# Six runs of four scatters, each begun at a step of the dense part, in place of three runs of eight

## The chip, the cores and the metric

The kernel runs on one core of a Trainium2 chip. The metric is the device time in microseconds of one execution; the time of the kernel before is the median of three.

## The reference

The input x is 8 batches of 256 rows, 128 wide. Three sub-layers follow, each on a layer norm of x without weights, each added back:

```python
x = x + 0.5 * ffn(layernorm(x))
x = x + attention(layernorm(x))
x = x + 0.5 * ffn(layernorm(x))
```

The FFN is a mixture of 8 experts with 2 chosen for each row: `gelu(x @ w1[e]) * (x @ v1[e])`, 352 wide, then `@ w2[e]`, weighted by the two largest of the softmax of `x @ router_w`, plus a bias. The attention has 16 heads of width 8, rotary positions and a linear distance term; it bears on the change only by what it waits for.

## The kernel before, in words

The rows are 16 tiles of 128 (`NT`). In the first FFN the first four tiles (`DT`) take the dense way: all eight experts are computed for them and weighted by the gate, 0 for an expert that was not chosen. The other twelve are routed: their normalised rows are scattered to a table in HBM (`xs0`), sorted by expert, each row twice (k is 0 or 1), and computed afterwards in blocks of 128 rows of one expert.

The engines run programs of their own, written out by hand, and meet by semaphores. Each engine executes in program order, so a wait holds everything behind it on that engine.

**The dense part** is a loop of 24 steps (i, three for each expert). In a step PE computes da and dv (`dense_up`, lines 1434 to 1436, two times three matmuls of 512 columns), ACT takes the gelu of da (`dense_gelu`, L842, waits for `da_full` and `dhid_done`), DVE multiplies it by dv (`dense_hid`, L1107, increments `dhid_done`; every fourth result goes to `vaug`, the others to `scr`; the third step of each expert is 96 rows high), and two steps later PE multiplies by w2 (`dense_down`, L1444). Between the steps stand LN, transposes, the routing of chunks c = 1 to 3 of four tiles (the last operation of each is `pos_done`, L1015), the block table of the first FFN on DVE (its last operation, `tab_e`, L1050), and ACT's near_high. After step 23 PE first does `xbT(0)` (L1462, transposes of the first three blocks), for which it waits until three block loads have landed, and only then the last two `dense_down`.

**GpSimd** in that time, in program order: LN's small operations, the first `add_ffn_bias` (half of the FFN's bias added to four tiles of xres, L593), then for c = 1 to 3 the eight scatters of a chunk (L531, two for each tile, each an indirect DMA of 128 rows), then `zero_scatter(0)` (L573 and L576, rows of zeros behind each expert's last row), then the other three bias adds. After that it waits for `scat1`, `zero_landed`, `spare_landed` and `tab`, clears the buffers of the attention with six memsets (L649, `zero_done`), sets `vaug` to 1 (L651, after `down_done` 24), and does `rstd_of(1, 0)` and `rstd_of(1, 1)` (L516 to L521), the attention's LN of the first tiles, which waits for DVE's statistics; then one scatter of results for each block (L538).

**SP** waits at `rows_there(0)` for the table, the scatters (`scat1`) and the zero rows (`zero_landed`) and then loads blocks (L418), six ahead. After the load for block 7 it waits for `zero_done`. **ACT** uses the result of `rstd_of(1, 0)` (`nmr_done`) in `ln_at(0)` (L736) after block 2. The bias adds are needed by `combine`, in the attention part.

Of the kernel before, what the change touches and what calls it, by code (L numbers as in the profile page):

```python
# [28 lines left out]
DT = 4  # L29
# [48 lines left out]
CHUNKS = [(4, 4), (2, 8)]  # L78


ROUTED = [CHUNKS[0][1], SPLIT, CHUNKS[1][1]]


# [38 lines left out]
def macaron(nc, x, small_w, w1, v1, w2, ffn_bias, proj_b, slopes, ident, dist, dist_t, rope, expert_ids,  # L122
            far, ones_rows, out):
    ctx = ExitStack()
    with ctx:
# [5 lines left out]
        def sem(name):  # L131
            return ctx.enter_context(nc.semaphore(name))

        def sems(name, n):
            return [ctx.enter_context(nc.semaphore(f"{name}{i}")) for i in range(n)]
# [21 lines left out]
        xn1 = qk_f[:, 6096:6096 + (NT - DT) * 2 * XW].rearrange("p (t k w) -> p t k w", t=NT - DT, k=2)  # L157
# [115 lines left out]
        def routing_bank(c):  # L273
# [32 lines left out]
        scat1, scat2 = sem("scat1"), sems("scat2", 2)  # L306
# [3 lines left out]
        da_full, dv_full, dgelu_done, dhid_done, down_done, dacc, xd_step, gd_step = (sem(n) for n in (  # L310
            "da_full", "dv_full", "dgelu_done", "dhid_done", "down_done", "dacc", "xd_step", "gd_step"))
# [20 lines left out]
        def rt_at(r, c, step):  # L332


            per = 2 * CHUNKS[r][0] + 6
            return c * per - (3 if r == 0 and c else 0) + (per if step is None else step)
# [13 lines left out]
        def loaded(engine, table, g, most):  # L350
            _, vals = nc.values_load_multi_w_load_instructions(
                table[0:1, g, :], engines=[engine], min_val=0, max_val=most,
                skip_runtime_bounds_check_because="the table's values are held in range by how it is made")
            return vals[0:GS]
# [156 lines left out]
        def _(pool):  # L511
# [11 lines left out]
            def scatter(r, c, src, landed, tiles=None):  # L523

                T = CHUNKS[r][0]
                p = 2 if r and c >= SPLIT else r
                pool.wait_ge(pos_done[r], c + r)
                pool.wait_ge(again_done[r], c + r)
                for t in tiles or range(c * T, (c + 1) * T):
                    for k in range(2):  # L530
                        nc.gpsimd.indirect_dma_start(  # L531
                            out=xs[p][:, :], out_offset=bass.IndirectOffsetOnAxis(ap=pos[:, k, t:t + 1], axis=0),
                            in_=src(t, k), in_offset=None).then_inc(landed, 16)
# [35 lines left out]
            def zero_scatter(p):  # L569
                r, zeros = min(p, 1), zero_rows2 if p else zero_rows1  # L570
                pool.wait_ge(zstep[r], 18 if p == 2 else 9)
                pool.wait_ge(numbered, 4 if p else 3)
                nc.gpsimd.indirect_dma_start(  # L573
                    out=xs[p][:, :], out_offset=bass.IndirectOffsetOnAxis(ap=zpos[:, 0, :], axis=0),
                    in_=zeros[:, ZG, :], in_offset=None).then_inc(zero_landed[r], 16)
                nc.gpsimd.indirect_dma_start(  # L576
                    out=xs[p].rearrange("(g z) d -> g (z d)", z=ZG),
                    out_offset=bass.IndirectOffsetOnAxis(ap=zpos[:, 1, :], axis=0),
                    in_=zeros[:, 0:ZG, :].rearrange("p z w -> p (z w)"), in_offset=None).then_inc(zero_landed[r], 16)
# [7 lines left out]
            def add_ffn_bias(r, q):  # L587
                if q == 0:
                    if r == 0:
                        nc.gpsimd.tensor_scalar(hbias[:, :], hbias[:, :], 0.5, None, ALU.mult).then_inc(half_done, 1)  # L590
                        pool.wait_ge(half_done, 1)
                pool.wait_ge(xn_done[2 * r], 4 * q + 4)
                nc.gpsimd.tensor_tensor(xres[:, 4 * q:4 * q + 4, :], xres[:, 4 * q:4 * q + 4, :],  # L593
                                        hbias[:, None, :].broadcast_to([P, 4, D]), ALU.add).then_inc(bias_added, 1)
# [41 lines left out]
            nc.gpsimd.tensor_scalar(slope8[:, :], slope8[:, :], 8.0, None, ALU.mult).then_inc(slope_done, 1)  # L636
            pool.wait_ge(numbered, 3)
            for c in range(1, 4):
                scatter(0, c, lambda t, k: xn1[:, t - DT, k, :], scat1)
            zero_scatter(0)  # L640
            for q in range(1, 4):
                add_ffn_bias(0, q)

            pool.wait_ge(scat1, 16 * 2 * (NT - DT))
            pool.wait_ge(zero_landed[0], 32)
# [323 lines left out]
        def _(dve):  # L969
# [51 lines left out]
            def block_table(p, step):  # L1021
# [3 lines left out]
                if step == 0:  # L1025
                    dve.wait_ge(rt[r], rt_at(r, ROUTED[p], 0))
                    nc.vector.tensor_tensor(T.tgt, end[:, :, None].broadcast_to([P, E, 16]), thr[:, :, :], ALU.is_gt
# [25 lines left out]
            def zero_rows(p):  # L1053


                r, at = min(p, 1), 9 if p == 2 else 0
                dve.wait_ge(rt[r], rt_at(r, ROUTED[p], 0))
                if p:
# [706 lines left out]
```

## Time and profile before

| | us |
|---|---|
| median of 3 runs | 485.16 |
| lowest and highest | 484.56, 487.63 |
| profiled execution, span from first to last instruction | 502.7 |
| PE busy, in the profiled execution | 441.0 |
| DVE, ACT, POOL busy | 311.2, 248.2, 237.4 |

The profiled execution is a single one, recorded by the hardware profiler. Its own time beyond the span isn't given; the span alone is 17.5 us more than the median. Rows give times in us from the span's start. "idle before" is what an engine waited before an instruction, with what ended the wait; "remote" and "issue" stand where the profile knows no instruction of this core that did.

### The profile page before, as it was taken

The page shows a single profiled execution, that of the slowest core. Times are in us where ns is not written, and L with a number is a line of the kernel's source. Part 1 is how long each engine was busy: PE and PEld are TensorE (multiplying, and loading weights), DVE is VectorE, ACT ScalarE, POOL GpSimd, SP SyncE. Part 2 cuts the span into 40 slices and gives each one's busy share as a digit, 9 for nine tenths or more (in the row PEclk, how much of TensorE's full clock was granted, in tenths as well). Part 3 has the DMA queues.
Part 4 walks back from the last instruction along what each step waited for, and adds up shares of the span by engine and source line. Part 5 has one row for each costly group of instructions (what it writes and reads, how often), then busy time and mean ns, then how long its engine had stood idle before and what let it go on. Part 6 is the DMA issues. An engine that isn't in the chain of part 4 may idle for free.

```text
span 502.7 us, 10906 instructions
## 1 busy us (share of the span) xinstructions
PE 441.0 (88%) x3447; PEld 369.0 (73%) x3447; DVE 311.2 (62%) x935; ACT 248.2 (49%) x585; POOL 237.4 (47%) x321
## 2 busy tenths in 40 slices
PE   1998859899999898699999999999779969999990
PEld 1877648788899775577777777777459958888880
DVE  3765645976867485295959586756526744544672
ACT  4744434436444456255556565555465524554541
POOL 7365658556453413044454545432525467534441
PEclk9999959999999999899999999999999989999997
DMA  8971111122331010230212120200112223122522
GB/s 236 290 116 38 48 58 33 50 75 75 91 85 54 30 48 15 71 85 17 60 50 61 47 63 30 64 24 3 70 37 61 64 60 96 53 65 72 171 80 78
DMA packets 50633, 35.51 MB, mean 71 GB/s; under 512 B 5754, under 2 KB 47706, under 8 KB 50538
## 3 DMA queue, kind: packets, MB, share of 16 engines
q1 hardware_dynamic: 45140, 23.90, 18.9%
q0 software_dynamic: 4784, 10.54, 6.3%
q8 instruction: 30, 0.49, 0.4%
q10 hardware_dynamic: 656, 0.40, 0.3%
q14 instruction: 23, 0.19, 0.1%
HBM read 15.37 MB, written 13.01 MB: 56 GB/s over the span
## 4 chain that ended last, share of the span: by engine, by line
PE 65%; DVE 9%; issue 8%; ACT 5%; POOL 4%; DMA 3%; another core or an unknown queue 2%; ACTq 1%; SPq 1%; POOLq 0%; DVEq 0%
PE bank L1490 9%; PE bank L1483 6%; PE bank L1587 5%; PE bank L1472 5%; PE bank L1473 4%; PE bank L1474 4%; PE bank L1626 4%; PE bank L1611 4%; PE bank L1444 3%; PE bank L1590 2%; PE bank L1591 2%; PE bank L1462 2%; PE bank L1614 2%; PE bank L1434 2%
## 5 line engine op out<-in xcount | busy, mean ns | idle before, releaser
L538 POOL DMA_INDIRECT yp<-scr,dest x77 | 76.5, 994 | 90.8 <-ACT scr L770 71.1
L877 ACT ACTIVATE stage<-bank 128x512 f32<-128x512 f32 x128 | 74.6, 597 | 72.6 <-PE bank L1615 63.7
L1263 DVE TENSOR_REDUCE nm<-bank 128x2 f32<-128x512 f32 x128 | 84.0, 685 | 38.4 <-PE bank L1591 35.8
L1490 PE MATMUL bank<-wd,scr 128*128 (+1 forms) x462 | 64.9, 277 | 1.3 <-ACT scr L763 1.3
L1472 PE MATMUL bank<-wu,xbT 128*128 x154 | 63.1, 410 | 2.1 <-DVE xbT L1129 1.8
L1137 DVE COPY scr<-bank 128x256 f32<-128x256 f32 x77 | 32.5, 422 | 51.5 <-PE bank L1483 22.8
L1490 PEld LDWEIGHTS bank<-wd,scr 128*128 128x128 f32 (+1 forms) x462 | 60.7, 193 | 1.8 <-issue 1.7
L1587 PE MATMUL bank<-qk_rows 126*128 126x256 bf16 x256 | 50.8, 280 | 4.9 <-DMA qk_rows<-lev 4.2
L1611 PE MATMUL bank<-qk_rows 128*128 128x256 bf16 x256 | 50.3, 279 | 3.7 <-DMA qk_rows<-wd 3.0
L1473 PE MATMUL bank<-wu,xbT 128*128 x154 | 50.8, 330 | 0.0
L1474 PE MATMUL bank<-wu,xbT 128*128 x154 | 50.8, 330 | 0.0
L783 ACT ACTIVATE scr<-bank 128x352 f32<-128x352 f32 x77 | 35.7, 463 | 29.1 <-PE bank L1474 21.7
L1483 PE MATMUL bank<-idn,scr 128*128 128x128 f32 (+1 forms) x231 | 40.1, 283 | 10.0 <-ACT scr L770 8.7
L1614 PE MATMUL bank<-near_hi,idn_r 128*128 128x256 f32 x128 | 47.3, 369 | 0.0
L1590 PE MATMUL bank<-near_hi,idn_r 128*128 128x256 f32 x128 | 47.0, 367 | 0.0
L1156 DVE TENSOR_TENSOR scr<-bank,scr 128x352 f32<-128x352 f32 x77 | 40.1, 521 | 9.4 <-ACT scr L783 2.1
L763 ACT ACTIVATE scr<-bank 96x128 f32<-96x128 f32 x77 | 21.0, 273 | 47.9 <-DVE scr L1137 33.9
L1483 PEld LDWEIGHTS bank<-idn,scr 128*128 128x128 f32 (+1 forms) x231 | 25.1, 138 | 23.0 <-issue 14.7
L1615 PE MATMUL bank<-near_lo,idn_r 128*128 128x256 f32 x128 | 36.0, 281 | 0.0
L1591 PE MATMUL bank<-near_lo,idn_r 128*128 128x256 f32 x128 | 35.8, 280 | 0.0
L531 POOL DMA_INDIRECT xs<-qk_rows,pos x28 | 27.4, 980 | 15.9 <-issue 9.9
L1626 PE MATMUL bank<-stage,vaug 128*9 128x256 f32 x512 | 34.2, 385 | 0.4 <-ACT stage L877 0.4
(218 smaller groups left out, 949.3 us busy)
## 6 DMA issues: line engine op xcount, KB each, us to landing
qk_rows<-lev SPq DMA_DIRECT2D x96, 64.0 KB
scr<-xs SPq DMA_DIRECT2D x77, 64.5 KB
stage<-yp SPq DMA_DIRECT2D x8, 256.0 KB, 3.2
scr<-yp SPq DMA_DIRECT2D x6, 256.0 KB, 3.1
stage<-in_w SPq DMA_DIRECT2D x8, 176.0 KB, 3.4
stage<-in_v SPq DMA_DIRECT2D x8, 176.0 KB, 4.3
xs<-qk_rows SPq DMA_DIRECT2D x3, 451.5 KB
yp<-scr,dest POOLq DMA_INDIRECT x77
```

The source lines that it names most:

```text
L538: nc.gpsimd.indirect_dma_start(out=yp[PHASE[n]][:, :], out_offset=bass.IndirectOffsetOnAxis(ap=dest[:, n:n + 1], axis=0), in_=ysb[:, n % Y ...
L877: nc.scalar.activation(probs[:, g % RING, kt, 2 * (hp % 2):2 * (hp % 2) + 2, :], psS2[(b * 16 + j) % 3][:, :].rearrange("p (h n) -> p h n" ...
L1263: nc.vector.tensor_reduce(nm[:, qt, 2 * hp:2 * hp + 2], psS1[i % 2][:, :].rearrange("p (h n) -> p h n", h=2), AX.X, ALU.max, negate=True). ...
L1472: nc.tensor.matmul(dst, hi, moving(n, a), start=True, stop=False)
L1473: nc.tensor.matmul(dst, lo, moving(n, a), start=False, stop=False)
L1474: nc.tensor.matmul(dst, hi, moving(n, a + 2 * F), start=False, stop=True).then_inc(done, 1)
L1483: i = nc.tensor.transpose(ph[n % len(ph)][0:w, k * P:(k + 1) * P], hid[:, n % 2, f:f + w], idn[:, :])
L1490: i = nc.tensor.matmul(ph[n % len(ph)][:, 3 * P:4 * P], hTs[0:w, n % 2, k * P:(k + 1) * P], wd[0:w, bass.ds(experts[n], 1), k, :].rearrang ...
L1587: nc.tensor.matmul(o[:, j * N:(j + 1) * N], qs[b % RING][0:S1_ROWS, h, qt * P:(qt + 1) * P], ks[b % RING][0:S1_ROWS, h, :], start=(j == 0) ...
L1590: nc.tensor.matmul(o, idn_r[:, :], near_hi[0][:, 2 * hp:2 * hp + 2, :], start=False, stop=False)
L1611: nc.tensor.matmul(o[:, a * N:(a + 1) * N], ks[b % RING][0:S2_ROWS, h, kt * P:(kt + 1) * P], qs[b % RING][0:S2_ROWS, h, :], start=(a == 0) ...
L1614: nc.tensor.matmul(o, idn_r[:, :], near_hi[1][:, 2 * hp:2 * hp + 2, :], start=False, stop=False)
```

## The change

The eight scatters of a chunk are split into two runs of four (two tiles each). Six runs, called turns 0 to 5 here, result. Each but the first waits until `dhid_done` has reached 5 + 3 x turn, that is 8, 11, 14, 17 and 20: dense steps 7, 10, 13, 16 and 19 are then done on DVE. After the first run of each chunk stands the chunk's bias add, so the three bias adds no longer follow the zero scatter. The zero scatter follows the sixth run directly.

```diff
+RUN_AT, RUN_STEPS = 5, 3
...
             for c in range(1, 4):
-                scatter(0, c, lambda t, k: xn1[:, t - DT, k, :], scat1)
+                for half in range(2):
+                    turn = 2 * (c - 1) + half
+                    if turn:
+                        pool.wait_ge(dhid_done, RUN_AT + RUN_STEPS * turn)
+                    scatter(0, c, lambda t, k: xn1[:, t - DT, k, :], scat1, range(4 * c + 2 * half, 4 * c + 2 * half + 2))
+                    if half == 0:
+                        add_ffn_bias(0, c)
             zero_scatter(0)
-            for q in range(1, 4):
-                add_ffn_bias(0, q)
```

Before, GpSimd from the first scatter of the routed tiles to the first memset (xs0 is the sorted table in HBM, pos and zpos the positions that rows go to):

```order
L531 DMA xs0<-qk_rows,pos 19712x129 [waits again_done0,pos_done0,numbered]
L531 DMA xs0<-qk_rows,pos 19712x129 x7
L531 DMA xs0<-qk_rows,pos 19712x129 [waits again_done0,pos_done0]
L531 DMA xs0<-qk_rows,pos 19712x129 x7
L531 DMA xs0<-qk_rows,pos 19712x129 [waits again_done0,pos_done0]
L531 DMA xs0<-qk_rows,pos 19712x129 x7
L573 DMA xs0<-qk_rows,zpos 19712x129 [waits numbered,zstep0]
L576 DMA xs0<-qk_rows,zpos 2464x1032
L593 TENSOR_TENSOR xres<-xres,hbias 128x512 [waits xn_done_f1] x3
L649 MEMSET qk_rows 128x2048 [waits spare_landed,tab0,zero_landed0,scat1]
```

After, the same engine from the rest of the third run (turn 2) to the same memset:

```order
L532 DMA xs0<-qk_rows,pos 19712x129 x3
L594 TENSOR_TENSOR xres<-xres,hbias 128x512 [waits xn_done_f1]
L532 DMA xs0<-qk_rows,pos 19712x129 [waits again_done0,pos_done0,dhid_done]
L532 DMA xs0<-qk_rows,pos 19712x129 x3
L532 DMA xs0<-qk_rows,pos 19712x129 [waits again_done0,pos_done0,dhid_done]
L532 DMA xs0<-qk_rows,pos 19712x129 x3
L594 TENSOR_TENSOR xres<-xres,hbias 128x512 [waits xn_done_f1]
L532 DMA xs0<-qk_rows,pos 19712x129 [waits again_done0,pos_done0,dhid_done]
L532 DMA xs0<-qk_rows,pos 19712x129 x3
L574 DMA xs0<-qk_rows,zpos 19712x129 [waits numbered,zstep0]
L577 DMA xs0<-qk_rows,zpos 2464x1032
L654 MEMSET qk_rows 128x2048 [waits spare_landed,tab0,zero_landed0,scat1]
```

Each run of four has its own wait for `dhid_done` now, a bias add stands behind the first run of each chunk, and nothing is left between the zero scatter and the memset. The other engines' programs are unchanged.

## Rows read from the trace of the kernel before

**Rows 1.** Page: the span, and the granted clock of PE in 40 slices

```profile
span 502.7 us, 10906 instructions
...
PEclk9999959999999999899999999999999989999997
```

**Rows 2.** Waits, 13 to 93 us: who for whom, us in total, times, longest

```profile
ACT scr L842 <- remote: 14.6, 3, 7.0
...
PE bank L1434 <- issue: 6.6, 2, 4.9
...
PE bank L1434 <- ACT scr L842: 1.2, 1, 1.2
```

**Rows 3.** Timeline of GpSimd (start, us, engine, line, operation, tiles, count, idle before)

```profile
24.36 1.64 POOL L593 TENSOR_TENSOR xres<-xres,hbias 128x512 f32<-128x512 f32 x1
...
42.38 0.95 POOL L531 DMA_INDIRECT xs<-qk_rows,pos  x1 [3.63 <-DVE pos L1015]
...
54.87 0.96 POOL L531 DMA_INDIRECT xs<-qk_rows,pos  x1 [2.33 <-DVE pos L1015]
...
66.23 0.95 POOL L576 DMA_INDIRECT xs<-qk_rows,zpos  x1 [0.31 <-issue]
67.20 3.73 POOL L593 TENSOR_TENSOR xres<-xres,hbias 128x512 f32<-128x512 f32 x3
77.50 10.55 POOL L649 MEMSET qk_rows<- 128x2048 f32 x6 [6.57 <-DVE tab_e L1050]
90.24 0.82 POOL L651 MEMSET vaug<- 128x864 f32 x1 [2.18 <-PE bank L1444]
92.88 0.28 POOL L516 TENSOR_SCALAR rstd<-mv 128x2 f32<-128x2 f32 x1 [1.82 <-DVE mv L976]
...
94.64 0.24 POOL L516 TENSOR_SCALAR rstd<-mv 128x2 f32<-128x2 f32 x1
```

**Rows 4.** Timeline of ACT: the gelu of step 16, and ln_at(0)

```profile
66.99 0.60 ACT L842 ACTIVATE scr<-bank 128x512 f32<-128x512 f32 x1 [6.98 <-remote]
...
96.68 0.87 ACT L736 ACTIVATE stage<-xres,nmr,rstd 128x128 f32<-128x128 f32 x2
```

**Rows 5.** Timeline of PE: end of da(16), the resumption, xbT(0), the other long idle

```profile
60.73 0.39 PE L1436 MATMUL bank<-xbT,wu 128*128 128x512 f32 x1
...
67.64 0.74 PE L1434 MATMUL bank<-xbT,wu 128*96 128x512 f32 x1 [4.95 <-issue]
...
87.90 0.49 PE L1462 MATMUL bank<-idn,scr 128*128 128x128 f32 x3
...
411.23 0.87 PE L1483 MATMUL bank<-idn,scr 128*128 128x128 f32 x3 [4.39 <-ACT scr L770]
```

**Rows 6.** By stretch: busy PE, PEld, DVE, ACT, POOL; PEclk, DMA share, GB/s

```profile
62.00:68.00 6.00, 1.05 (x8) 0.86 (x7) 0.00 (x0) 1.01 (x3) 4.76 (x6) 0.77 0.18 63
68.00:76.00 8.00, 7.31 (x24) 5.43 (x24) 5.29 (x11) 3.20 (x8) 2.94 (x3) 0.53 0.13 52
```

**Rows 7.** Timeline of DVE: a cast, the table's last operation, dense_hid(19)

```profile
24.78 1.26 DVE L993 CAST ixf<-ix 128x8 f32<-128x8 uint32 x1
...
76.98 0.38 DVE L1050 TENSOR_REDUCE tab_e<-qk_rows 1x33 int32<-1x231 f32 x1
78.10 0.69 DVE L1107 TENSOR_TENSOR vaug<-bank,scr 128x512 f32<-128x512 f32 x1 [0.74 <-ACT scr L842]
```

**Rows 8.** Bytes moved, 40 slices each: of 67 to 77 us, then of 78 to 83

```profile
GB/s 0 0 17 429 396 429 429 380 33 0 0 0 0 0 0 0 0 0 0 0 0 0 0 0 0 0 0 0 0 0 0 0 0 0 0 0 0 0 0 0
...
GB/s 0 0 0 0 0 0 0 0 37 186 186 108 17 87 157 136 79 112 128 227 112 17 0 12 144 219 103 156 70 140 161 116 62 165 161 103 37 0 8 8
```

**Rows 9.** Timeline of SP: the first block loads

```profile
78.08 12.12 SPq L418 DMA_DIRECT2D scr<-xs  x7
```

**Rows 10.** Busy time by stretch: about 411 us, and the first expert blocks

```profile
410.00:418.00 8.00, 6.78 (x33) 6.64 (x33) 2.97 (x9) 2.54 (x8) 3.83 (x4) 0.57 0.34 116
88.00:100.00 12.00, 10.78 (x79) 9.66 (x77) 11.05 (x38) 5.06 (x15) 6.87 (x12) 1.00 0.20 52
```

## The prediction

> **What bounds the kernel now.** I read the page first: span 502.7 us, PE busy 88% of it [rows 1]. So PE's idle stretches and its slow-clock stretches are the only places where much can be won. The waits of the dense part (13 to 93 us) come next: ACT's gelu waits 14.6 us in three stretches for something that the profile can't name, the longest 7.0, and PE loses 6.6 us in two stretches and 1.2 in one behind it [rows 2]. GpSimd's timeline shows what goes on meanwhile: three unbroken series of indirect DMAs, eight scatters each, the second from 42.38 and the third from 54.87 us, the last with the two zero scatters right behind it [rows 3]. From 54.87 to 66.23 there are nine steps, so one scatter costs 11.36 / 9 = 1.262 us of GpSimd.
>
> The worst stall in detail: PE ends the last of da(16) about 61 us (its L1436 at 60.73), the gelu that needs it starts at 66.99, and PE, which needs that gelu, resumes at 67.64 after 4.95 us [rows 4, 5]. No semaphore of the kernel explains the 6 us: the gelu waits for da_full and dhid_done, both in. It happens only inside long series of scatters. Then the clock: PEclk 0.77 in 62 to 68 us and 0.53 in 68 to 76, that is mostly the 1.2 GHz level after 4.95 us without a matmul [rows 6]; 7.31 us of PE work there at 0.53 cost 7.31 x 0.47 = 3.4 us. After the two shorter idles of PE the clock stays full (nines in the page's PEclk row up to the slice of 62.8 to 75.4 us, a 5) [rows 1].
>
> **What the change does to the stalls.** Sum of what stands in the trace: 6.6 + 1.2 us of PE idle + 3.4 us of clock = 11.2 us. The new runs are four scatters, 4 x 1.262 = 5.0 us, with a bias add or a wait between. The stalls of before set in some 5 to 7 us into a series, so the trace of after should have none, or little, in the first five runs. Price if the stalls are real: -11.2 us.
>
> **What it adds.** The last run now waits for dhid_done 20, the end of dense_hid(19). That is the DVE row at 78.10 that writes vaug; it ends at 78.79 [rows 7]. From there, in the frame of before, where steps 19 to 23 run without a stall:
> - wake-up 0.2 us (estimate), four scatters and two zero scatters without a pause: 5 x 1.262 + 0.95 = 7.3. Together 7.5.
> - the zero scatter's data: its instruction at 66.23 ends at 67.18, its last bytes move at about 69.2 (ninth bin of 0.25 us after 67) [rows 3, 8]: 2.0.
> - SP stands at rows_there for zero_landed and then loads. Before, the table was the last to come: tab_e ends at 77.36, SP's first issue is at 78.08 [rows 7, 9]: 0.7.
> - three loads of 64.5 KB: the zero among the bytes at about 80.7 us ends the first three of six [rows 8, 9]: 80.75 - 78.08 = 2.7.
> Sum 12.9 us after dhid(19). PE wants these three tiles for xbT(0) at 87.90 [rows 5], 87.90 - 78.79 = 9.1 after it. Before, the loads lay there at about 81, 7 us early. Now PE stands for 12.9 - 9.1 = **3.8 us**, with the last two dense_down, dense_add and everything after them queued behind. All the slack of the rows' path is used, and 3.8 more.
>
> The second follower is GpSimd itself: six memsets of qk_f wait for zero_landed as well (10.55 us from 77.50), then vaug (0.82), then rstd_of(1, 0), which at 92.88 waited for DVE's statistics [rows 3]. From dhid(19): 9.5 (zero landed) + 10.6 + 0.9 + 1.7 for its four operations (the next group starts at 94.64) = 22.7, so nmr is there at 101.5; ACT used it at 96.68 [rows 4]. That is 4.8 us late, 1.0 beyond the 3.8 of PE; if PE's slow clock costs that 1.0 anyway it is hidden. Slack before: 92.88 against 91.06, 1.8 us. zero_done for SP's ones_rows has the same 10.6 us before it, but its readers come later still, behind the 3.8; I charge nothing.
>
> Clock after the new idle: nothing in the trace shows this place idle. Bounds: 0 (the idles of 1.6 and 1.2 us left the clock full) and 3.4 (the 4.95 us idle). The nearest row is the 4.39 us idle of PE before 411.23: the window from 410 to 418 us has 0.57 with PE busy 6.78 us [rows 5, 10], so 6.78 x 0.43 = 2.9 us. In the expert blocks PE is busy about nine tenths (10.78 of 12 us, rows 10), so I take 2.5, both ends kept. Added: 3.8 + 2.5 = **6.3 us**, not under 4.8 (the GpSimd path alone), not over 7.2.
>
> **Other edits.** The bias adds (3.73 us for three) leave the place between zero scatter and memset, where they hid under landing and table; moving them out saves GpSimd nothing that ends last. In the dense part they may hold DVE: at 24.78 a cast of 128x8 took 1.26 us while the first bias add ran [rows 3, 7]. Two of the new places have such small DVE operations, none of them on PE's path for more than a fraction: between 0 and 1.2 us, I take 0. The Trainium skill (SBUF — State Buffer, Who interferes with whom) says that GpSimd and a DVE cast or an operation with two SBUF inputs exclude each other for a whole instruction; the cast's row agrees, and by it three collisions could be had where one was.
>
> **Which frame counts.** In the frame of the profile the sum is -11.2 + 6.3 = -4.9 us, a span of about 498. But the profiled execution is not the timed one: its span alone is 502.7, the median 485.16, so 17.5 us, with whatever lies around the span, are missing in the timed runs. The matmul stretches can't give much of that, since they run at the granted clock with no gap; it is most easily found in the unexplained gaps: 11.2 here, and 4.39 + 2.9 about 411 us, behind a series of indirect DMAs as well, sum 18.5. So my likeliest case is that the timed runs have little of these stalls. Then the change removes nothing that they paid, and the 6.3 us are paid: 485.2 + 6.3 = **491.5 us**. The trace of after would get shorter while the time gets longer. The Trainium skill (Runtime: NRT & Kernel Launch, The ~15µs preamble/postamble breakdown) has a profile's total some 6.2 us above the execution time for an epilogue; first to last instruction holds no epilogue, so by that rule the 17.5 us here stay unexplained.
>
> **Rivals.**
> 1. The stalls are in every execution, and the 17.5 us are spread over thousands of traced instructions (10906, rows 1). For: ACT's gelu stands for 6 us with its inputs there, and nothing marks this as the profiler's. Against: the 17.5 us, and that the three stalls and the one at 411 us sum to just that. Mechanism: GpSimd's series over some five scatters hold up ACT between gelu(8) and gelu(16); price 11.2 us; it decides as soon as the timed runs hold more than 6.3 us of it. Then 485.2 - 11.2 + 6.3 = 480.3 us; 477 if the clock does not fall at xbT(0).
> 2. About half of the stall is in the timed runs: -5.6 + 6.3, 486 us, not told from no change.
> 3. The rows' path has more slack in the timed runs (landing or loads faster) or the clock holds: 485.2 + 3.8 or 4.8, 489 to 490, without the stalls.
> 4. The change doesn't do what it says: four in a row stall ACT too. The attention part has runs of four without such a gap, which speaks against; then the stalls stay and the delay comes on top, some 491.
>
> **How the numbers follow.** Forecast 0.42 (own range 489.5 to 494), rival 1 0.32, rival 2 0.11, rival 3 0.11, rival 4 0.04. One per cent (4.9 us), about what a measurement of this kernel tells from no change, is 480.3 below and 490.0 above. Rival 1 lies on the lower line: three quarters of it beyond, as some of its stall gaps (0.7 us of a slow gelu, smaller idles) are not in my 11.2, gives 0.24, and 0.01 from elsewhere. Slower: 0.37 of the forecast's 0.42, 0.03 of rival 4, 0.02 of rival 3: 0.42. The rest, 0.33, is within 1%. Range 477 to 494: low end rival 1 with the clock held, high end the forecast with 3.4 us of clock and one collision.
>
> **What would show it.** In the trace of after: no unnamed wait of gelu over 2 us before the last run (stall step right); the zero scatters about 7.5 us behind dhid(19); SP's first load some 10 us behind it; PE idle 3 to 5 us before L1462's new line, released by a DMA; PEclk near 0.5 for some microseconds after it; the first memset right at the landing, and nmr of tile 0 late for ACT. If PE has no idle at xbT(0), the added part is wrong. If the median falls by as much as the trace's sum, rival 1 is right and my reading of the 17.5 us wrong.

## The result and the profile after

| | before | after |
|---|---|---|
| median us (lowest to highest) | 484.86 (484.32 to 487.63), 4 runs | 492.33 (491.26 to 493.66), 4 runs |
| ratio, 95% interval | | 1.0167, 1.0127 to 1.0207 |

The change costs 7.5 us, 1.7%. 491.5 was forecast. Here and in the experiments, ratios and intervals leave out a run that lies more than 1.5% above the fastest of its kernel. The profiled execution of after took 491.79 us, its span is 489.9: 1.9 us lie outside the span. The first profile of before, at 502.7, was not a usual execution (below); the undisturbed one of before shown here and there is the first experiment's, span 482.4.

A view that is said to be "to [rows n]" is to be compared with that group of rows of before. Page of after, to [rows 1]:

```profile
span 489.9 us, 10909 instructions
...
PEclk9999997999999999999999899999998999999996
```

Waits of after, 13 to 93 us (who for whom, us in total, times, longest), to [rows 2]:

```profile
ACT scr L847 <- PE bank L1441: 23.6, 21, 3.6
...
PE bank L1467 <- DMA scr<-xs: 5.6, 1, 5.6
...
POOL qk_rows L654 <- issue: 2.5, 1, 2.5
```

No gelu waits for something unnamed any more. PE has one new wait, for the block loads. GpSimd's timeline of after (start, us, engine, line, operation, tiles, count, idle before), to [rows 3]:

```profile
63.56 1.29 POOL L594 TENSOR_TENSOR xres<-xres,hbias 128x512 f32<-128x512 f32 x1
66.09 1.39 POOL L532 DMA_INDIRECT xs<-qk_rows,pos  x1 [1.23 <-DVE vaug L1112]
...
72.83 0.96 POOL L577 DMA_INDIRECT xs<-qk_rows,zpos  x1 [0.30 <-issue]
76.28 10.56 POOL L654 MEMSET qk_rows<- 128x2048 f32 x6 [2.49 <-issue]
...
89.12 0.20 POOL L522 TENSOR_TENSOR nmr<-nmr,rstd 128x2 f32<-128x2 f32 x1
```

DVE of after, the table and dense_hid(19), to [rows 7]:

```profile
63.05 1.86 DVE L1053 TENSOR_TENSOR tab_r<-qk_rows,ig 1x33 int32<-1x33 f32 x1
64.84 0.37 DVE L1055 TENSOR_REDUCE tab_e<-qk_rows 1x33 int32<-1x231 f32 x1
65.14 0.67 DVE L1112 TENSOR_TENSOR vaug<-bank,scr 128x512 f32<-128x512 f32 x1
```

SP, PE and ACT of after, one fence each, to [rows 9], [rows 5] and [rows 4]:

```profile
77.03 6.87 SPq L419 DMA_DIRECT2D scr<-xs  x7
```

```profile
73.51 1.05 PE L1449 MATMUL bank<-wd,scr 128*128 128x128 f32 x8
80.16 0.88 PE L1467 MATMUL bank<-idn,scr 128*128 128x128 f32 x3 [5.60 <-DMA scr<-xs]
80.83 1.92 PE L1449 MATMUL bank<-wd,scr 128*128 128x128 f32 x8
```

```profile
91.08 0.87 ACT L741 ACTIVATE stage<-xres,nmr,rstd 128x128 f32<-128x128 f32 x2
```

Busy time of after by stretch (PE, PEld, DVE, ACT, POOL; PEclk, DMA share, GB/s), to [rows 6]:

```profile
78.00:80.00 2.00, 0.00 (x0) 0.00 (x0) 0.00 (x0) 0.00 (x0) 2.00 (x3) 0.50 0.39 103
80.00:82.00 2.00, 1.84 (x9) 1.87 (x10) 0.34 (x1) 0.49 (x1) 2.00 (x2) 0.50 0.39 95
82.00:84.00 2.00, 2.00 (x11) 2.00 (x11) 1.33 (x2) 0.00 (x0) 2.00 (x2) 0.50 0.00 0
84.00:86.00 2.00, 1.69 (x10) 1.40 (x8) 1.43 (x5) 0.46 (x1) 2.00 (x2) 0.83 0.31 79
```

Read as a chain: dense_hid(19) ends at 65.81 and lets the sixth run go at 66.09; the last zero scatter ends at 73.79, its rows have landed at 76.28, SP loads from 77.03, and at 80.16 PE has its three blocks, 5.60 us after it could have begun. Then PE works at a granted clock of 0.50 from 80 to 84 us and of 0.83 on average from 84 to 86. Its busy time in each stretch, times the share of the clock that is missing, is 1.84 x 0.50 + 2.00 x 0.50 + 1.69 x 0.17 = 2.2 us. 5.6 + 2.2 = 7.8 us.

### The profile page after: what moved, and what is told of

It reads as the page before. It is cut to its first block, busy times and chain, and to the rows that moved or that the text cites. A ratio compares the mean times of both kernels' runs of the same rounds, so it can differ in the third digit from the quotient of the medians.

```text
span 489.9 us, 10909 instructions
## 1 busy us (share of the span) xinstructions
PE 436.0 (89%) x3447; PEld 365.2 (75%) x3447; DVE 316.6 (65%) x935; ACT 247.9 (51%) x585; POOL 239.0 (49%) x321
## 4 chain that ended last, share of the span: by engine, by line
PE 50%; issue 8%; DVE 7%; DMA 7%; ACT 5%; POOL 5%; SPq 2%; ACTq 1%; DVEq 0%; POOLq 0%
PE bank L1495 6%; PE bank L1592 5%; PE bank L1488 5%; PE bank L1631 4%; PE bank L1616 4%; PE bank L1477 4%; PE bank L1478 3%; PE bank L1479 3%; PE bank L1595 2%; PE bank L1596 2%; POOL yp L539 2%; PE bank L1619 2%; PE bank L1620 2%; PE bank L1467 2%; DMA qk_rows<-wd 2%
## 5 line engine op out<-in xcount | busy, mean ns | idle before, releaser
L532 POOL DMA_INDIRECT xs<-qk_rows,pos x28 | 28.7, 1026 | 17.7 <-issue 9.0
```

## Experiments

Kernels that were measured together share a chip and the runs of before beside them. Times are medians, ratios are to before. Theory A in the expectations is the forecast's: the date of the last run and what follows it in series make PE stand at xbT(0). The other letters are explained where they appear.

**1. Before once more, for its profile**

> The kernel before, unchanged, with a fresh profile. Theory A (the rows arrive late; the unnamed gelu waits of the first profile were not in the timed executions): 485 us, ratio 1.00, and a span near 483 in which PE idles under 2 us in one piece between 25 and 77 us. Theory B (the scatter series of eight hold up ACT in every execution, and the change removes that): gelu waits of 3 to 7 us again, 11 us in sum. The time is 485 in both; the profile decides.

Measured: 483.87 us (10 runs; before beside it 485.71, 25 runs), ratio 0.9966, interval 0.9937 to 0.9996: two sets of runs of one kernel may differ by 0.3%. Profiled execution 484.32 us, span 482.4. Waits, GpSimd, DVE and PE of this profile:

```profile
ACT scr L842 <- PE bank L1436: 24.4, 22, 3.6
```

```profile
58.30 1.23 POOL L531 DMA_INDIRECT xs<-qk_rows,pos  x1 [0.30 <-issue]
...
61.11 0.96 POOL L576 DMA_INDIRECT xs<-qk_rows,zpos  x1 [0.31 <-issue]
62.09 3.76 POOL L593 TENSOR_TENSOR xres<-xres,hbias 128x512 f32<-128x512 f32 x3
66.36 10.55 POOL L649 MEMSET qk_rows<- 128x2048 f32 x6 [0.50 <-DVE tab_e L1050]
```

```profile
62.83 3.08 DVE L1048 TENSOR_TENSOR tab_r<-qk_rows,ig 1x33 int32<-1x33 f32 x1
```

```profile
66.86 0.47 PE L1434 MATMUL bank<-xbT,wu 128*96 128x512 f32 x1 [1.31 <-DVE vaug L1107]
...
74.50 1.05 PE L1444 MATMUL bank<-wd,scr 128*128 128x128 f32 x8
75.39 0.49 PE L1462 MATMUL bank<-idn,scr 128*128 128x128 f32 x3
```

Theory A holds. Eight scatters in a row, and more, stall nothing here: no gelu has an unnamed wait, and xbT(0) follows dense_down without idle. The three stalls of [rows 2] did not come again. None of the 75 other timed runs of before (481.95 to 488.43 us) had a time near 502.7. And a loss shows that the first profile had hidden: tab_r on DVE, an operation of the block table, takes 3.08 us against 0.18 in it. It falls beside the bias adds on GpSimd here (62.09 to 65.85 us); that they hold it up is what experiments 5, 10 and 11 show.

**2. The change without its waits**

```diff
-                    if turn:
-                        pool.wait_ge(dhid_done, RUN_AT + RUN_STEPS * turn)
```

> The change without its waits for dhid_done: runs of four, bias adds between. Theory A: nothing is late, 485 us (484 to 486.5). Theory C (the bias adds and scatters inside the dense part hold up DVE or ACT, whenever they start): still 488 to 492.

Measured: 484.79 us, ratio 0.9987 (0.9953 to 1.0021), as theory A has it; C falls. Runs of four with bias adds between them cost nothing as a whole that the interval would show, so the waits are the loss. One thing is left open: ACT waits 1.63 us for nmr at ln_at(0) in this profile and in that of experiment 3, since the memsets begin late behind a late landing of the zero rows (last section), and neither median shows it.

**3 and 4. The last run at step 16, and at step 21**

```diff
-RUN_AT, RUN_STEPS = 5, 3
+RUN_AT, RUN_STEPS = 2, 3
```

and, in the other kernel, 7, 3.

> All turns three steps earlier (5, 8, 11, 14, 17 instead of 8 to 20). Theory A: the last run ends about 7 us earlier, more than the 5.6 us that PE idled before xbT(0): idle gone, 485 us (484 to 486.5). Theory C: as after, 492. A middle value of 487 to 489 would say that GpSimd's memset path or bias collisions have a share.

> All turns two steps later (10, 13, 16, 19, 22). Theory A: dense_hid(21) ends 4.1 us after dense_hid(19) in the profile of after, so PE idles 9.7 us before xbT(0) and the time is 492.3 + 4.1 = 496.4 us (495.5 to 498). Theory C: no more than the changed kernel, 492.

Measured: 483.9 us over ten runs (481.66 to 489.06), ratio 0.9977 (0.9941 to 1.0013), and 495.74 us over four, ratio 1.0203 (1.0147 to 1.026). Theory A holds, the early one a little under its range (484 to 486.5); C falls. Same waits in number, another date. PE at xbT(0) in the early and in the late one:

```profile
74.94 0.52 PE L1467 MATMUL bank<-idn,scr 128*128 128x128 f32 x3 [0.27 <-DMA scr<-xs]
```

```profile
84.49 0.88 PE L1467 MATMUL bank<-idn,scr 128*128 128x128 f32 x3 [9.34 <-DMA scr<-xs]
```

PE's idle is 0.27, 5.60 and 9.34 us for the last run at dense step 16, 19 and 21, and the time goes with it. At step 16 the rows come only 0.27 us late, although their zero rows took 1.7 us longer to land than in after (4.2 against 2.5, last section).

**5. Only the last of the five waits**

```diff
-                    if turn:
+                    if turn == 5:
```

> The kernel after with one wait for dhid_done left of five, the one before the sixth run (20). Theory A (all of the loss comes from the date of the last run): the same time as after, 492 us, ratio 1.014 to 1.018, PE idle 5 to 6 us before xbT(0). Theory B (part of the loss comes from the other waits, which leave the earlier scatters late or put them beside DVE's small operations): under 491 us, by at least 1 us. Theory C (an execution with the stalls of the first profile is brought about by how closely scatters follow each other): the stalls of gelu, unnamed, over 2 us, come back in this profile.

Measured: 489.56 us (12 runs; before beside it 485.44, 29 runs), ratio 1.0086 (1.0053 to 1.0118). Theory A alone fails here: 2.8 us less than after (492.33), where it forecast no difference, and the intervals of the two ratios lie apart. Theory B holds in size; C falls, no unnamed wait came back although the first 20 scatters follow each other without a wait for dhid_done. What differs:

```profile
63.01 0.18 DVE L1053 TENSOR_TENSOR tab_r<-qk_rows,ig 1x33 int32<-1x33 f32 x1
```

```profile
73.14 1.05 PE L1449 MATMUL bank<-wd,scr 128*128 128x128 f32 x8
79.09 0.59 PE L1467 MATMUL bank<-idn,scr 128*128 128x128 f32 x3 [4.89 <-DMA scr<-xs]
```

The last bias add lies at 56.71 us here, before the table's operations, and tab_r is not held. To compare profiles I take one operation of ACT, in which the kernels do not differ yet, as zero. It is called the mark below. The undisturbed before and after have it at 37.85 and 37.31 us:

```profile
37.85 0.60 ACT L741 ACTIVATE qk_rows<-bank 128x512 f32<-128x512 f32 x1 [0.84 <-PE bank L1422]
```

```profile
37.31 0.60 ACT L746 ACTIVATE qk_rows<-bank 128x512 f32<-128x512 f32 x1 [0.84 <-PE bank L1427]
```

Here it stands at 38.03. The last dense_down ahead of xbT(0) starts 36.65 us after the mark in before, 36.20 in after, 35.11 here. So a bias add beside tab_r delays the dense part by 1.5 us in before and 1.1 in after. In experiments 3 and 4 tab_r takes 0.18 us too, so the step from experiment 3 to after holds this 1.1 beside the idle. PE's idle is 0.7 shorter as well: 1.1 + 0.7 = 1.8 at xbT(0). The clock is 0.85, 0.50 and 0.80 in the stretches of two microseconds from 78 us (PE busy 0.91, 2.00, 1.99), which makes 1.5 us in place of 2.2. 1.8 + 0.7 = 2.5 of the 2.8; the rest is within the spread of the runs.

**6. Dummy transposes that keep PE's clock**

```diff
                 pe.wait_ge(tab[r], 10)
+                if r == 0:
+                    for k in range(WARM):
+                        nc.tensor.transpose(bank[7][:, (k % 4) * P:(k % 4 + 1) * P], idn[:, :], idn[:, :])
```

> The kernel after, with 48 dummy transposes (128x128, into a bank of PSUM that is free then, nobody reads them) on PE between the wait of dense step 23 and xbT(0). They last some 5.3 us and fill the idle of PE there. Theory A (5.6 us are the missing rows, some 2.2 us are the slow clock after the idle): PEclk stays at 1.00 through 78 to 86 us and the time falls by 2.2 us against after, to about 490; xbT(0) itself begins at the same moment, released by the loads. Theory D (the clock costs nothing, since the rows after xbT(0) wait for something else, such as GpSimd's path to ln_at(0)): 492, no change.

WARM is 48. Measured: 492.8 us over 12 runs. The ratio, 1.0114 (1.0071 to 1.0156), rests on ten of them, whose median is 491.66. These ten lie in two groups, five from 487.29 to 490.65 us and five from 492.67 to 493.98. The clock is 1.00 in every stretch from 74 to 90 us, and the profiled run took 490.65, 1.1 less than after's. At ln_at(0) a second wait had been right behind:

```profile
91.45 0.88 ACT L742 ACTIVATE stage<-xres,nmr,rstd 128x128 f32<-128x128 f32 x2 [1.63 <-POOL nmr L523]
```

ln_at(0) of the undisturbed before, for comparison:

```profile
84.18 0.87 ACT L736 ACTIVATE stage<-xres,nmr,rstd 128x128 f32<-128x128 f32 x2
```

From the mark, ln_at(0) is at 53.77 in after (91.08 - 37.31), 53.63 here (91.45 - 37.82), 46.33 in before (84.18 - 37.85). PE is ahead by 1.9 us: its third group of up matmuls behind xbT(0) starts at 84.54 - 37.82 = 46.72, against 85.91 - 37.31 = 48.60 in after. ACT gives most of this away again to GpSimd's chain. The median of the ten is 0.7 us under after's, and the two intervals overlap, so theory D is not refuted by times.

**7. Zero scatter before the last run**

```diff
+                    if turn == 5:
+                        zero_scatter(0)
                     if turn:
...
-            zero_scatter(0)
```

> The kernel after, with the zero scatter put before the wait of the sixth run in place of behind it. Theory A (what follows dense step 19 in series sets xbT(0): 4 scatters, 2 zero scatters, landing, loads): the two zero scatters, 1.26 + 0.95 = 2.2 us, leave the chain, and the landing of a plain scatter may be shorter than that of the zero rows (2.3 us): 2.2 to 4 us less, 488 to 490. Theory E (SP's loads wait for something else, a table or the earlier rows): 492.

Measured: 487.85 us, ratio 1.0045 (1.0015 to 1.0075): 4.5 us less than after, a little more than the 2.2 to 4 of theory A. GpSimd and PE:

```profile
72.42 0.96 POOL L532 DMA_INDIRECT xs<-qk_rows,pos  x1 [0.30 <-issue]
74.78 10.56 POOL L655 MEMSET qk_rows<- 128x2048 f32 x6 [1.40 <-DMA xs<-qk_rows,pos]
```

```profile
78.53 0.59 PE L1468 MATMUL bank<-idn,scr 128*128 128x128 f32 x3 [3.52 <-DMA scr<-xs]
```

A plain scatter lands in 1.40 us, the zero rows in 2.49 (in after). But the zero scatters begin only at 65.47, behind a bias add, and push the last run to 68.63. So from the end of dense_hid(19) to the landing it takes 8.5 us here (74.78 - 66.27) and 10.5 in after (76.28 - 65.81), 2.0 less. PE's idle is 2.1 us shorter and its clock is 0.71, 0.50, 0.93 in the 2 us windows from 78 (PE busy 1.48, 2.00, 1.73): 1.6 us in place of 2.2. That makes 2.7 of the 4.5, and ln_at(0) does stand 2.6 sooner after the mark (88.90 - 37.77 = 51.13). The profiled runs differ by 3.7; what the rest is stays open. Theory E falls.

**8. One memset of six ahead of the last run**

```diff
+                    if turn == 5:
+                        nc.gpsimd.memset(qk_f[:, 2048:4096], 0.0).then_inc(zero_done, 1)
...
-            for i in range(2 * RING):
+            for i in (0, 2, 3, 4, 5):
```

> The kernel after, with one of the six memsets (1.76 us) put before the wait of the sixth run, where GpSimd stands idle anyway, so that nmr of tile 0 is ready 1.8 us sooner. Theory A (PE's wait for the rows is what costs, GpSimd's second path is hidden behind it): no change, 492. Theory F (the path memsets, vaug, rstd_of(1, 0), ln_at(0) sets the loss): 1.8 us less, 490.2.

Measured: 491.81 us, ratio 1.0133 (1.0088 to 1.0178), six runs; profiled 491.91 against 491.79. No change is seen. The interval alone would also hold theory F's 1.8 us less; the profile decides. nmr is ready at 89.46 us and used at 91.58, and ln_at(0) stands 53.97 us after the mark (91.58 - 37.61), no sooner than in after. Alone, GpSimd's second chain is hidden behind PE's idle and slow clock, as forecast.

**9. Both together: transposes and early memset**

> The kernel after with both edits together: the dummy transposes on PE before xbT(0), and one of the six memsets before the wait of the sixth run. With the transposes alone ACT waited 1.6 us for nmr of tile 0, so that only some 1.4 of the 2.2 us of slow clock came back up to there; with the memset alone nothing did. Theory A with the second path right behind: no wait of ACT at ln_at(0), and about 1 us less than with the transposes alone, a profiled run of 489.5 or less. Theory D (the clock is worth nothing): 491.5 or more. Timed runs of the transposes alone lay in two groups, about 488.5 and 493; if they do so here too, the two groups are compared apart.

Measured: 493.03 us, ratio 1.0146 (1.0098 to 1.0194); six runs, 487.56, 491.10, and four from 492.85 to 493.49. The profiled one is of the upper group, 493.35 us. The wait at ln_at(0) is gone, and ln_at(0) comes 1.6 us sooner than with transposes alone (89.86 - 37.84 = 52.02 after the mark, against 53.63): up to there both halves work. The gain is lost some 315 us later, in the second FFN, on ACT, PE and in the clock:

```profile
408.45 0.28 ACT L778 ACTIVATE scr<-bank 128x128 f32<-128x128 f32 x1 [2.73 <-DMA yp<-scr,dest]
```

```profile
408.87 0.52 PE L1491 MATMUL bank<-idn,scr 128*128 128x128 f32 x3 [2.53 <-ACT scr L778]
```

```profile
408.00:412.00 4.00, 3.13 (x17) 3.09 (x18) 0.95 (x2) 1.29 (x5) 3.79 (x4) 0.74 0.30 82
412.00:416.00 4.00, 4.00 (x26) 3.63 (x25) 1.72 (x4) 1.67 (x6) 3.64 (x4) 0.83 0.05 16
```

After has no idle of PE over 1 us there (0.85 at the same place) and a clock of 1.00. So 1.7 us of idle and 3.13 x 0.26 + 4.00 x 0.17 = 1.5 us of clock come in here, 3.2 in all. The profiled run is 1.6 us longer than after's though it was 1.75 ahead at ln_at(0), a loss of 3.3. ACT waits for a result scatter that stands behind the second zero scatter, and this zero scatter lands late here (last section). The profile of transposes alone has the same late landing and 2.30 us of idle, with the clock at 1.00. What parts the two groups is thus not settled: there is one profile in each. The profiled run missed the forecast (489.5 or less); one timed run of six met it.

**10. The bias adds back behind the zero scatter, waits kept**

> The kernel after, with its five waits kept and the three bias adds back behind the zero scatter. Theory G (in after a bias add holds up DVE's tab_r and with it dense step 19, 1.86 us against 0.18): tab_r takes 0.18 us, dense_hid(19) and everything behind it come about 1.1 us sooner, so 491.2 against 492.3, ratio about 1.013; the bias adds (3.8 us) last beyond the landing of the zero rows (2.5 us) and push the memsets by 1.2 us, hidden by the 1.8 us that nmr of tile 0 had to spare. Rival, the prediction's term (moving the bias adds is worth nothing): 492.3, ratio 1.015 to 1.017.

Measured: 491.75 us, ratio 1.015 (1.0113 to 1.0187), six runs, not told from after. tab_r takes 0.18 us, and the last dense_down stands at 35.11 after the mark, as theory G says. But the memsets are later against DVE, and another operation is caught:

```profile
80.85 6.74 DVE L1136 COPY dest<-scr 128x3 uint32<-128x3 uint32 x1
```

```profile
87.83 0.52 PE L1488 MATMUL bank<-idn,scr 128*128 128x128 f32 x3 [3.08 <-DVE scr L1161]
```

A copy of 128x3, 0.16 us when alone, lasts 6.74 us: to 87.59, the end of the memsets and of vaug's (87.56) on GpSimd. In after it takes 1.20. PE waits 3.08 us for what follows it, and its clock falls once more (0.76 from 88 to 90 us, 0.50 from 90 to 92). The 1.1 us won at tab_r is lost here and more: ln_at(0) stands 55.39 us after the mark (93.15 - 37.76), 1.6 later than in after. Where the profiled run, 0.2 us shorter than after's, makes this good was not followed. The interval holds both theories' ratios: G's tab_r came true, its gain in the total is not shown.

**11. Before with its bias adds behind the memsets**

```diff
             zero_scatter(0)
-            for q in range(1, 4):
-                add_ffn_bias(0, q)
...
                 nc.gpsimd.memset(qk_f[:, i * 2048:(i + 1) * 2048], 0.0).then_inc(zero_done, 1)
+            for q in range(1, 4):
+                add_ffn_bias(0, q)
             pool.wait_ge(down_done, 3 * E)
```

> The kernel before, with nothing of the change, but its three bias adds moved from behind the zero scatter to between the six memsets and the memset of vaug, where GpSimd has about 1 us of idle and would have 3 more. In before they hold DVE's tab_r for 3.08 us in place of 0.18, and PE stands 1.3 us for it. Theory G: tab_r 0.18 us, no such wait of PE, the table 2.7 us sooner, 1 to 1.5 us less: 484 where before is 485.4, ratio 0.997. Rival (the delay is made good in the stall-free steps behind it, or GpSimd's path to nmr is late by the 3.8 us instead): 485.4 or more.

Measured: 481.63 us (480.13 to 486.7, 12 runs; before beside it 484.21, 17 runs), ratio 0.9944 (0.9912 to 0.9976). That is 2.6 us less than before and 10.7 less than after's median. The interval lies below 1, but so did that of experiment 1, where a kernel was compared with itself and differed by 0.34%; so the gain rests on the profile as well. Its GpSimd, DVE and PE:

```profile
64.86 10.55 POOL L647 MEMSET qk_rows<- 128x2048 f32 x6 [2.48 <-DMA xs<-qk_rows,zpos]
75.38 3.75 POOL L593 TENSOR_TENSOR xres<-xres,hbias 128x512 f32<-128x512 f32 x3
79.07 0.82 POOL L651 MEMSET vaug<- 128x864 f32 x1
```

```profile
63.14 0.18 DVE L1048 TENSOR_TENSOR tab_r<-qk_rows,ig 1x33 int32<-1x33 f32 x1
```

```profile
73.27 1.05 PE L1444 MATMUL bank<-wd,scr 128*128 128x128 f32 x8
```

tab_r is free, dense_down at 73.27 - 38.16 = 35.11 after the mark, 1.54 sooner than in before, and ln_at(0) at 82.98 - 38.16 = 44.82 against 46.33: the 1.5 us are kept. Theory G holds. The rest of the 2.6 lies within the interval.

## Why the prediction was right, and where its terms were off

**Which frame counts: right in result, wrong in wording.** The likeliest case was that timed runs hold little of the 11.2 us of stalls. The profile of experiment 1, an execution from among the timed ones, holds none. But "the profiled execution is not the timed one" is not so: every other profiled execution lies among the timed ones, 1.9 us above its span. The 502.7 us were one odd execution. Rivals 1 and 2 are refuted by experiments 1 and 2, rival 4 by after's waits. What held up ACT in that execution is open: it did not come again (one trace of it is in the last section).

**PE's idle at xbT(0): right mechanism, 3.8 forecast, 5.6 measured.** Its terms:

| | forecast us | measured us |
|---|---|---|
| wake-up and six scatters | 7.5 | 8.0 (73.79 - 65.81; the first scatter after the wait lasts 1.39, not 0.96) |
| landing of the zero rows | 2.0 | 2.5 |
| SP's first load after it | 0.7 | 0.75 |
| three loads | 2.7 | 3.1 (80.16 - 77.03) |
| sum | 12.9 | 14.35 |
| what PE had to do meanwhile | 9.1 | 8.75 (80.16 - 5.60 - 65.81) |

So the sum was 1.45 too small and PE's work 0.35 too large. The four durations were each read a little short from rows of another place, all in one direction. The landing shows how: the forecast ended it with the last bytes, but the wait for it ended some 0.5 us later.

**Clock 2.5: right, 2.2 measured.** Experiment 6 shows it at 1.00 where PE is kept busy, but not that it is worth 2.2 us in the median. For the sum there is a check: ln_at(0) stands 53.77 - 46.33 = 7.4 us later after the mark in after than in the undisturbed before.

**Moved bias adds, taken as 0: off.** The first profile had tab_r at 0.18 us, since the stalls had pushed the table (tab_e at 76.98, [rows 7]) behind the bias adds, which end at 70.93 [rows 3]; so the loss that stood at the old place was not seen. In a usual execution of before they cost 1.5 us, in after 1.1. So the move gained 0.4: 5.6 + 2.2 - 0.4 = 7.4, where 7.5 was measured.

**GpSimd's second chain: hidden, as forecast.** nmr is ready at 89.32 and used at 91.08, 1.8 us to spare; experiment 8 gets nothing from it, experiment 6 runs into it. From dense_hid(19) it took 23.5 us, 22.7 were forecast. Two of the signs that the forecast named failed all the same: nmr was to be late for ACT and was not, since PE came later than forecast, and PE's idle, 5.6 us, lies above the 3 to 5.

**Rival 3** (loads faster, or the clock holds) fell: landing and loads were slower, the clock fell. Part of the closeness is luck: 1.8 us too little idle stood against 0.3 too much clock and 0.4 of gain left out. 6.3 and 7.5 differ by 1.2; 491.5 and 492.33 only by 0.8, as before's median fell from 485.16 to 484.86. A slip in the sums changed nothing: rival 1 with the clock held is 480.3 - 2.5 = 477.8, not 477.

## What to carry to other kernels

Before spreading or dating transfers, work out the chain behind the last one (issue, landing, the queue that loads, the loads) and compare it with the time until the consumer wants them; only slack beyond that may be used. A single profile that lies 17 us above the timed runs should be taken anew before any stall in it is worked on. Small vector operations on a critical chain belong where GpSimd is idle; look for one operation whose duration differs many times between two profiles.

## What the runs showed of the hardware

- DVE against GpSimd: tab_r (two inputs of 1x33 in SBUF) takes 0.18 us alone, 1.86 beside one bias add and 3.08 beside three in a row; the copy of 128x3 took 0.16 alone, 1.20 beside the memsets in after and 6.74 in experiment 10. Each time it ended within 0.1 us of the end of a GpSimd instruction, in the last case only after several memsets and vaug's. The Trainium skill (SBUF — State Buffer, Who interferes with whom) has a DVE copy, in a mode that uses two ports, and GpSimd exclude each other: the one that issues first holds the shared ports for a whole instruction. The copy of after agrees, it ends with the memset in which it began. In experiment 10 it was held through the four GpSimd instructions behind that one as well, and tab_r in the undisturbed before through all three bias adds. Why it was passed over there and not in after is open.
- In after tab_r begins at 63.05, half a microsecond before the bias add's row at 63.56, and is held all the same; no run explains this. In experiments 2 and 3 it took 0.18 us beside a scatter that no bias add follows.
- Landing of the zero rows, from the end of the instruction: 2.5 us in after and in experiments 4 to 6, 8, 9 and 11, but 4.3 and 4.2 in experiments 2 and 3. In experiment 1 the last bytes move 1.9 us after the instruction, as in after. In experiments 2 and 3, and in none of the others named, the fetch of a piece of program (queue q8) falls among the zero rows. Bytes and queues in 40 slices of 65 to 70.7 us of experiment 2, and of 72.5 to 76.4 us of after:

```profile
GB/s 29 406 29 0 0 0 0 0 0 0 0 0 0 348 435 377 435 377 435 348 406 406 173 0 0 0 0 0 0 29 0 0 29 0 29 0 0 0 0 0
...
q0 software_dynamic: 176, 0.59, 27.2%
q8 instruction: 1, 0.02, 1.0%
```

```profile
GB/s 0 0 0 0 0 0 466 212 0 0 0 0 0 0 0 0 0 0 42 466 423 339 423 381 466 466 339 466 381 423 423 339 43 0 0 0 0 0 0 0
...
q0 software_dynamic: 176, 0.59, 38.3%
```

  The same 176 packets; with the one of q8 among them, a few stragglers come 0.9 to 1.6 us behind the rest. It falls among the second FFN's zero rows, or at their end, in experiments 6 and 9 (within the half microseconds from 404.0 and 406.0 us), where ACT and PE then stand. Ten dense parts agree, two with the fetch and eight without. But no run moved the fetch alone, and the second zero scatter's own instruction lasts 1.45 us in place of 0.96 in experiments 2 and 3, so the fetch is a candidate for the cause.
- The stalls of the odd execution: a piece of program (queue q14) arrives within the half microseconds from 35.5, 46.0 and 61.0 us in it. Two of the three lie in the stalls of gelu that end at 40.18 and 66.99. In the undisturbed before such pieces come at 35.5, 43.5 and 56.0 and stall nothing. A piece from q8 arrives within the half microsecond from 49.0, where the third stall sets in (49.20 to 52.39); three of q8's in the undisturbed before stall nothing. So late program is a candidate, not a finding.
- The clock: 5.60 us without a matmul took it to 0.50 for some four and a half microseconds of the work that followed; it was there too after 4.89 us in experiment 5 and 3.52 us in experiment 7 (0.50 from 80 to 82 us in both) and after the 3.08 us of experiment 10 (0.50 from 90 to 92 us). After the 9.34 us of experiment 4 it was at 0.50 in every stretch from 84 to 90 us.
